# Double-buffering the token-tile operands of the K/V and Q projection loops

## The reference

```python
z = _layernorm(x)                       # (8, 2048, 1024), eps 1e-5
q, k, v = heads(Wq, bq), heads(Wk, bk), heads(Wv, bv)   # z @ W + b, 16 heads of 64
eq = jax.nn.elu(q)
ek = jax.nn.elu(k)
qn = eq / jnp.linalg.norm(eq, axis=-1, keepdims=True)
kn = ek / jnp.linalg.norm(ek, axis=-1, keepdims=True)
kv = jnp.einsum('bhsd,bhse->bhde', kn, v)
ctx = jnp.einsum('bhsd,bhde->bhse', qn, kv) / jnp.float32(math.sqrt(HD))
attn_out = _layernorm(ctx @ Wo + bo + z, g1, be1)
h = _gelu(attn_out @ W1 + b1)
out = _layernorm(h @ W2 + b2 + attn_out, g2, be2)
x = x + out                             # then a second layer: ternary-weight FFN with relu^2
```

## Time and profile before

| | us |
|---|---|
| median of the 2 runs shown | 6860.17 |
| lowest and highest of them | 6643.05, 7077.29 |
| the profiled execution's own time | 6654.75 |
| its span (slowest core, core 7) | 6653.2 |
| spans of the 8 cores | 6626.1 to 6653.2 |
| mean granted PE clock, all cores | 0.813 to 0.815 of full speed |

### The profile page before, as it was taken

How to read it: one execution, slowest core, us unless ns; L and a number is a source line. 1 busy time by engine, 2 the same in 40 slices (tenths; PEclk the granted TensorE clock), 3 DMA queues, 4 the chain that set the end, 5 groups by cost and what they waited for, 6 DMA issues and landing times.

```text
span 6653.2 us, 49468 instructions; the slowest of 8 cores (6626.1 to 6653.2 us)
## 1 busy us (share of the span) xinstructions
PE 3820.2 (57%) x16008; PEld 1598.1 (24%) x16008; DVE 1610.1 (24%) x2032; ACT 1075.9 (16%) x1151; POOL 169.4 (3%) x228
## 2 busy tenths in 40 slices
PE   1004555344458579699599599500001977768596
PEld 1001222121123034244134144000000322323232
DVE  2442222323330230120220220133233203121220
ACT  2000111112100121130130120221100403113040
POOL 0130000000000000000000000000000000000000
PEclk9998777677669789799799799755555998989899
DMA  2571000000000033143143132011221221212122
GB/s 91 173 232 68 0 0 0 29 0 0 0 26 0 0 87 94 44 97 96 40 90 100 40 91 85 0 65 65 73 63 40 52 50 51 50 47 53 45 54 57
DMA packets 649506, 374.35 MB, mean 56 GB/s; under 512 B 549328, under 2 KB 582304, under 8 KB 648240
## 3 DMA queue, kind: packets, MB, share of 16 engines
q1 hardware_dynamic: 629296, 304.07, 17.3%
q0 software_dynamic: 19968, 67.12, 3.2%
HBM read 312.39 MB, written 58.72 MB: 56 GB/s over the span
## 4 chain that ended last, share of the span: by engine, by line
PE 54%; DVE 16%; DMA 16%; issue 8%; ACT 6%; DVEq 1%; SPq 0%; ACTq 0%; POOLq 0%; POOL 0%
PE ps_p L1202 10%; PE ps_h L1140 10%; PE ps_h L1677 7%; PE ps_y L1748 5%; DMA ph8w<-spill_pj 4%; PE ps_q L489 3%; PE ps_v L489 3%; PE ps_wo L888 3%; PE ps_k L489 2%; DMA ph<-x 2%; PE ps_h L1680 2%; DMA spill_w1p<-phwp 2%; DMA spill_w2p<-phwp 2%; DMA strB<-wfc 2%; DMA spill_pj<-strB 2%
## 5 line engine op out<-in xcount | busy, mean ns | idle before, releaser
L1140 PE MATMUL ps_h<-ph 128*128 128x512 bf16 x3072 | 680.1, 382 | 51.0 <-DVE ph L1102 35.4
L1202 PE MATMUL ps_p<-strB,ph 128*128 128x512 bf16 x3072 | 674.2, 383 | 31.2 <-DMA ph<-spill_w2p 31.2
L1748 PE MATMUL ps_y<-strB,ph8w 128*128 128x512 bf16 x2048 | 491.8, 387 | 177.9 <-DMA ph8w<-spill_pj 138.1
L489 PE MATMUL ps_v<-ph1w,ph1zp 128*128 128x512 bf16 x768 | 201.5, 430 | 631.5 <-DVE ph1zp L479 631.5
L1677 PE MATMUL ps_h<-ph,ph8w 128*128 128x512 bf16 x2048 | 474.2, 385 | 14.3 <-DMA ph8w<-spill_fc 14.3
L1140 PEld LDWEIGHTS ps_h<-ph 128*128 128x128 bf16 x3072 | 296.6, 98 | 434.1 <-issue 94.8
L1202 PEld LDWEIGHTS ps_p<-strB,ph 128*128 128x128 bf16 x3072 | 302.8, 99 | 402.6 <-issue 48.0
L489 PE MATMUL ps_q<-ph1w,ph1zp 128*128 128x512 bf16 x768 | 201.9, 431 | 309.1 <-DVE ph1zp L479 309.1
L1694 ACT ACT_TABLE_LOAD x128 | 164.2, 1283 | 1069.1 <-PE ps_h L1680 1022.2
L1748 PEld LDWEIGHTS ps_y<-strB,ph8w 128*128 128x128 bf16 x2048 | 187.9, 99 | 483.2 <-issue 305.0
L1156 ACT ACT_TABLE_LOAD x128 | 164.2, 1283 | 735.2 <-PE ps_h L1140 735.2
(11 more groups left out here) (206 smaller groups left out, 3677.3 us busy)
## 6 DMA issues: line engine op xcount, KB each, us to landing
ph<-spill_w1p SPq DMA_DIRECT2D x256, 256.0 KB
ph<-spill_w2p SPq DMA_DIRECT2D x256, 256.0 KB
ph8w<-spill_fc SPq DMA_DIRECT2D x128, 256.0 KB
ph8w<-spill_pj SPq DMA_DIRECT2D x256, 128.0 KB
ph<-x SPq DMA_DIRECT2D x32, 512.0 KB
phwp<-w1t SPq DMA_DIRECT2D x32, 512.0 KB
spill_w1p<-phwp POOLq DMA_DIRECT2D x64, 256.0 KB, 3.9
phwp<-w SPq DMA_DIRECT2D x32, 512.0 KB
```

Of the source, the lines that this page charges most:

```text
L489: last = t.matmul(ps[:, cols], zz[:, k * 128:(k + 1) * 128], ww.rearrange("p (k w) -> p k w", k=ND)[:, k, cols], start=(pi == 0 and k == 0 ...
L1140: last = t.matmul(dst, ww[:, k * 128:(k + 1) * 128], aa[:, k, :], start=(pi == 0 and k == 0), stop=(pi == 2 and k == ND - 1))
L1202: last = t.matmul(ps_p2[:, n * 512:(n + 1) * 512], ww[:, n * 128:(n + 1) * 128], mm, start=(i == 0 and pi == 0), stop=False)
L1748: last = t.matmul(ps_y[:, jj * 512:(jj + 1) * 512], pjb[i % 2][:, jj * 128:(jj + 1) * 128], mm, start=(i == 0 and pi == 0), stop=(i == NF ...
```

## The change

- `zh`/`zl` get two buffers (`zpp`, `ph1zp` grows from 1024 to 2048 columns), one for even and one for odd tiles. The derive of tile `si + 1` moves ahead of the elu chain of tile `si` in DVE's list, behind the bias adds, and waits only for the projection that last read its buffer (`t_free`) in place of all matmuls.
- `kb` and `vb` get two buffers each; `bkb` moves from `B_t` to a tile of its own. `t_kv` keeps one count for each buffer.
- `e3` and `q3` are dropped: the max with 0 is done behind the exp and overwrites the buffer of the min, with a wait of its own, and the add follows.
- PE's wait on "s" ahead of a projection is dropped.
- SP gets a block that waits for the set-up's counts, and the loads of wv and wk lose their explicit wait for `v_z0`.

The diff, cut to its core:

```diff
+        setup_marks = {}
...
+        setup_marks["v"] = b.cnt["v"]
+        setup_marks["t"] = b.cnt["t"]
...
-        kb = B_t[:, 0:1024]
-        vb = B_t[:, 1024:2048]
-        e1 = B_t[:, 2048:3072]
-        e2 = B_t[:, 3072:4096]
-        e3 = B_t[:, 4096:5120]
+        kbp_ = [B_t[:, 0:1024], B_t[:, 2048:3072]]
+        vbp_ = [B_t[:, 1024:2048], B_t[:, 3072:4096]]
+        e1 = B_t[:, 4096:5120]
+        e2 = B_t[:, 6272:7296]
...
-                v.tensor_scalar(e1, blk, 0.0, None, ALU.min)
-                b.inc(v.tensor_scalar(e3, blk, 0.0, None, ALU.max), "v", 1)
+                b.inc(v.tensor_scalar(e1, blk, 0.0, None, ALU.min), "v", 1)
...
                 b.wait(v, "s", sv)
-                b.inc(v.tensor_add(e1, e2, e3), "v", 1)
+                b.inc(v.tensor_scalar(e1, blk, 0.0, None, ALU.max), "v", 1)
+                b.wait(v, "v")
+                b.inc(v.tensor_add(e1, e2, e1), "v", 1)
...
-        def derive_pair_blocks(zh, zl, si, v_ready):
+        def derive_pair_blocks(zh, zl, si, v_ready, t_free):
...
-            def _(v, v_ready=v_ready, t_e=t_e):
+            def _(v, v_ready=v_ready, t_free=t_free):
                 b.wait(v, "v", v_ready)
                 b.wait(v, "v")
-                b.wait(v, "t", t_e)
+                b.wait(v, "t", t_free)
                 b.inc(v.tensor_copy(zh3, srcs), "v", 1)
...
+            def _(sy):
+                b.wait(sy, "t", setup_marks["t"])
+                b.wait(sy, "v", setup_marks["v"])
+            block.sync(_)
+            v_wv = load_resident_w_pairs(wv_h, wv_l, wv_d, wtmp_kv)
+            v_wk = load_resident_w_pairs(wk_h, wk_l, wk_d, wtmp_kv)
-            v_wv = load_resident_w_pairs(wv_h, wv_l, wv_d, wtmp_kv, wait_v=v_z0)
-            v_wk = load_resident_w_pairs(wk_h, wk_l, wk_d, wtmp_kv, wait_v=v_z0)
...
+                dv[0] = derive_pair_blocks(zpp[0][0], zpp[0][1], 0, v_z0, 0)
...
                 for si in range(NT):
-                    sp, vp = derive_pair_blocks(zh, zl, si, v_z0)
-                    def _(t, si=si, v_evac_last=v_evac_last, sp=sp, vp=vp):
-                        b.wait(t, "v", max(v_wk, vp))
-                        b.wait(t, "s", sp)
+                    zh, zl = zpp[si % 2]
+                    def _(t, si=si, v_evac_last=v_evac_last, spvp=dv[si]):
+                        b.wait(t, "v", max(v_wk, spvp[1]))
                         if si >= 1:
                             b.wait(t, "v", v_evac_last)
                         tok_proj3(t, ps_v, wv_h, wv_l, zh, zl)
                         b.inc(tok_proj3(t, ps_k, wk_h, wk_l, zh, zl), "t", 1)
...
+                        v.tensor_add(vbp_[si % 2], ps_v[:], bvb)
+                        b.inc(v.tensor_add(kbp_[si % 2], ps_k[:], bkb), "v", 1)
                     v_evac_last = b.cnt["v"]
-                    v_elu[si] = elu_norm(kb)
+                    if si + 1 < NT:
+                        dv[si + 1] = derive_pair_blocks(
+                            zpp[(si + 1) % 2][0], zpp[(si + 1) % 2][1], si + 1,
+                            v_z0, t_proj[(si + 1) % 2])
+                    v_elu[si] = elu_norm(kbp_[si % 2])
```

More of the change, by code:

```diff
@@ L497, in build_program @@
         with nc.sbuf_tensor("ph1w", [128, 8192], F32) as WKV, \
-             nc.sbuf_tensor("ph1zp", [128, 1024], F32) as ZP:
+             nc.sbuf_tensor("ph1bias", [128, 1024], F32) as BKB, \
+             nc.sbuf_tensor("ph1zp", [128, 2048], F32) as ZP:
             WKVb = WKV[:].bitcast(BF16)
@@ L503, in build_program @@
             ZPb = ZP[:].bitcast(BF16)
-            zh, zl = ZPb[:, 0:1024], ZPb[:, 1024:2048]
+            zpp = [(ZPb[:, 0:1024], ZPb[:, 1024:2048]),
+                   (ZPb[:, 2048:3072], ZPb[:, 3072:4096])]
+            bkb = BKB[:]
             wtmp_kv = B_t[:, 0:2048]
@@ L575, in build_program @@
                 v_evac_last = 0
-                t_kv_last = 0
+                t_kv = [0, 0]
+                t_proj = [0, 0]
                 v_acc = 0
                 v_elu = [0] * NT
+                dv = [None] * NT
+                dv[0] = derive_pair_blocks(zpp[0][0], zpp[0][1], 0, v_z0, 0)
                 def emit_kv(si):
-                    nonlocal t_kv_last, v_acc
+                    nonlocal v_acc
                     def _(t, si=si, v_kn=v_elu[si], v_acc_=v_acc):
@@ L586, in _ @@
                             b.wait(t, "v", v_acc_)
+                        kb, vb = kbp_[si % 2], vbp_[si % 2]
                         last = None
@@ L597, in emit_kv, with _ @@
                     block.tensor(_)
-                    t_kv_last = b.cnt["t"]
-                    def _(v, si=si, tkv=t_kv_last):
+                    t_kv[si % 2] = b.cnt["t"]
+                    def _(v, si=si, tkv=t_kv[si % 2]):
                         b.wait(v, "t", tkv)
@@ L620, in build_program @@
                     block.tensor(_)
+                    t_proj[si % 2] = b.cnt["t"]
                     tp = b.cnt["t"]
@@ L624, in build_program, with _ @@
                         emit_kv(si - 1)
-                    def _(v, si=si, tp=tp, t_kv_last=t_kv_last):
+                    def _(v, si=si, tp=tp, tkv=t_kv[si % 2]):
                         b.wait(v, "t", tp)
                         b.wait(v, "ld", ld_b)
-                        b.wait(v, "t", t_kv_last)
-                        v.tensor_add(vb, ps_v[:], bvb)
-                        b.inc(v.tensor_add(kb, ps_k[:], bkb), "v", 1)
+                        b.wait(v, "t", tkv)
+                        v.tensor_add(vbp_[si % 2], ps_v[:], bvb)
+                        b.inc(v.tensor_add(kbp_[si % 2], ps_k[:], bkb), "v", 1)
                     block.vector(_)
                     v_evac_last = b.cnt["v"]
-                    v_elu[si] = elu_norm(kb)
+                    if si + 1 < NT:
[3 more added lines that the diff above has]
+                    v_elu[si] = elu_norm(kbp_[si % 2])
                 emit_kv(NT - 1)
@@ L652, in build_program @@
                 return nc
-            with nc.sbuf_tensor("ph1q", [128, 6400], F32) as PQ:
-                qbp = [PQ[:, 0:1024], PQ[:, 5376:6400]]
+            with nc.sbuf_tensor("ph1q", [128, 5376], F32) as PQ:
+                qbp = [PQ[:, 0:1024], PQ[:, 4352:5376]]
                 q1 = PQ[:, 1024:2048]
                 q2 = PQ[:, 2048:3072]
-                q3 = PQ[:, 3072:4096]
-                qrst = PQ[:, 4096:4224]
-                bq_pq = PQ[:, 4224:5248]
+                qrst = PQ[:, 3072:3200]
+                bq_pq = PQ[:, 3328:4352]
                 def elu_norm_q(blk):
@@ L667, in _ @@
                         b.wait(v, "v")
-                        v.tensor_scalar(q1, blk, 0.0, None, ALU.min)
-                        b.inc(v.tensor_scalar(q3, blk, 0.0, None, ALU.max), "v", 1)
+                        b.inc(v.tensor_scalar(q1, blk, 0.0, None, ALU.min), "v", 1)
                     block.vector(_)
@@ L680, in _ @@
                         b.wait(v, "s", sv)
-                        b.inc(v.tensor_add(q1, q2, q3), "v", 1)
+                        b.inc(v.tensor_scalar(q1, blk, 0.0, None, ALU.max), "v", 1)
+                        b.wait(v, "v")
+                        b.inc(v.tensor_add(q1, q2, q1), "v", 1)
                         b.wait(v, "v")
@@ L764, in emit_qtr, with _ @@
                         v_ev = b.cnt["v"]
+                    t_projq = [0, 0]
+                    dvq = [None] * NT
+                    dvq[0] = derive_pair_blocks(zpp[0][0], zpp[0][1], 0, v_kv, 0)
                     for si in range(NT):
[L767 to L771, removed]
+                        zh, zl = zpp[si % 2]
+                        def _(t, si=si, v_bias=v_bias, spvp=dvq[si]):
+                            b.wait(t, "v", max(v_wq, spvp[1]))
                             b.wait(t, "ld", ld_bq)
@@ L776, in build_program @@
                         block.tensor(_)
+                        t_projq[si % 2] = b.cnt["t"]
                         tp = b.cnt["t"]
@@ L787, in build_program @@
                         v_bias = b.cnt["v"]
+                        if si + 1 < NT:
+                            dvq[si + 1] = derive_pair_blocks(
+                                zpp[(si + 1) % 2][0], zpp[(si + 1) % 2][1], si + 1,
+                                v_kv, t_projq[(si + 1) % 2])
                         v_qn[si] = elu_norm_q(qbp[si % 2])
```

4 lines of the change are left out of this document (removed).

## The result

| us | before | after |
|---|---|---|
| median of all executions | 6878.01 (10) | 6314.3 (11) |
| lowest | 6643.05 | 6271.68 |
| the profiled execution's own time | 6654.75 | 6311.08 |
| its spans, lowest and highest core | 6626.1, 6653.2 | 6245.2, 6309.5 |
| ratio after to before | | 0.948, 95% interval 0.9435 to 0.9525 |

The medians of both kernels hold executions in which a die ran at a lower matrix clock for long, and the ratio leaves those out. The change makes the kernel 5.2% faster. The forecast was 6270 us, 0.942 of the profiled execution's 6654.75: the direction was right, the gain was forecast a little too large (385 us, while 0.948 leaves some 346), and 0.942 lies outside the measured interval. The range of 6225 to 6315 just holds the median of 6314.3; but set beside the median shown at the time, 6860.17, it ran from 0.907 to 0.921, and 0.948 is not in that.

What follows compares the result with a forecast made beforehand. PE was taken to wait at each K/V and Q handover for the derive queued behind the elu chain on DVE. Removing 194.9 us (K/V) and 189.9 (Q), 385 together, from 6654.75 gave 6270 us, range 6225 to 6315.

Steps and rivals of the forecast that it cites:

- The K/V loop: K/V handovers: the derive moved ahead of the elu chain removes 12.99 us from each of 15, 194.9 us.
- The cover: K/V loop: the 13 us chain hides under some 22.5 us of v and k matmuls, some 9 us to spare.
- The Q loop: Q handovers: 19.23 us for 31.93 in 14, with first handover and last tile 189.9 us removed.
- the rival limb: Q loop: the chain on DVE, 13.01 us, competes with PE's burst; it ends at 12.58 us from burst start.
- The clock at the start of a burst: Both loops: PE's idle shrinks from 18.6 to about 5.6 us, yet bursts start as slow as now, change 0.
- a rival with 5%: Both loops: the high clock survives the short idle, 32 us less, 6238 us; chance 5%.
- The weight loads: Set-up: they lose a wait that cost nothing and SP still issues right behind DVE's last copy; taken as 0.
- The sum: Both loops: 194.9 + 189.9 = 385 us off the profiled 6654.75, giving 6270 us.
- The dropped wait on "s": PE ahead of projections in 31 handovers: at most 0.1 us each, 0 to 3 us less; taken as 0.
- The clock under a denser load: All cores: rival that denser PE load brings a clock between the levels on the whole die, 6366 us; chance 3%.
- the estimate of 96 us: Both loops: by the skill's 13/16 limit, 16 tiles of 120 fast matmuls each take 0.05 us more per matmul.
- My range: Whole kernel: own range 6245 to 6300 us; widened to 6225 to 6315 to take in the high-clock rival, 88%.

Runs made afterwards that it cites:

- the overlapped version: Kernel after plus derive of tile si + 2 and accumulation or transpose copy inside the chain's waits, v taken out during k, two q PSUM buffers: ratio 0.9126.

## Why the prediction was right and where it was wrong

*The K/V loop:* right. Forecast 29.66 us a handover (42.65 less 12.99), measured 29.63 on core 7 and 29.6 to 29.8 on every core without the third level. The cover was there: the chain of a tile ends at 639.90 and `emit_kv`, which waits for it, starts at 650.54, 10.6 us later where some 9 were forecast, and without the chains the loop is no faster. Seen alone, 6460 us forecast and spans of 6460.2 to 6477.5 on the four unaffected cores.

*The Q loop:* right. Forecast 19.23 for 14 of the handovers, measured 19.24 on core 7 (1081.36 to 1350.68 us); with the shorter first one all 15 average 19.0 to 19.1 on the cores without the third level. The chain did become the rival limb. Its length with the moved max was forecast at 13.01 us and is 13.03. The Trainium skill (VectorE: DVE Perf Modes, section The DRAIN you can't avoid) says of a row of copies that the semaphore between them costs nothing extra; for this pair of operations the trace differs, if only by some 0.2 us. PE's second idle, before the transposes, is there in some tiles and up to 0.88 us long on core 7.

*The clock at the start of a burst:* right. The idle is 5.3 to 5.6 us and the next burst still starts at 1.2 GHz: the v halves of core 7 take 11.8 to 13.5 us and its k halves 10.5. That the high level outlasts the idle, a rival with 5%, didn't happen at these idles; in the overlapped version it held with no idle in K/V, and in some tiles of Q behind 2.84 us.

*The weight loads:* right. In the trace of after, on core 7, DVE's last copy ends 0.13 us before SP's first issue, to the hundredth as in the earlier trace rows, and the wv loads follow from 199.18 us on:

```profile
196.72 1.23 DVE L365 COPY strA<-ps_tr 128x1024 f32<-128x1024 f32 x1 [2.30 <-PE ps_tr L355]
198.08 0.33 SPq L53 DMA_DIRECT2D strB<-bv  x1
```

*The sum:* 385 us forecast, 383 found in the loops and 377 in the whole time, both without the third level. Of the 8 us, 2 are in the loops, 1 between them, and 5 were not placed. They are the smaller part of the miss: the eight executions of after that the ratio of 0.948 rests on average 6301.8 us, 32 over the forecast. The dropped wait on "s" was not tried alone; the handovers leave hardly 0.1 us for it.

*The clock under a denser load:* wrong, and this is the step that failed: the sum has no term for a clock between 1.2 and 2.4 GHz, and nothing was set aside for it in the range. I held the third level against the row in which 100 us of PE without a gap show 1.00 on core 7 and gave it 3%. That row was from an execution in which no core met the level, and one such execution can't tell how often it comes. Over all executions for which the cores' clocks are known, a die was below its usual clock in 26 of 32 of the kernel after and in 31 of 57 of the kernel before, some of them by very little. The profiled execution of after had it on four of eight cores, on two of these in both loops: 44 us in K/V and 12 in Q, so that the slowest core took 6309.5 us where core 0 took 6245.2. The time is that of the slowest of eight cores, so one pair is enough. With 377 us gained, an execution free of the level takes 6278 us, and the six of the kernel after in which no die was low took 6262.45 to 6291.9, 6278 on average. By the costs above, a pair caught in Q alone adds 12 and a pair caught in both loops 56, 6290 to 6334; the seven executions besides the profiled one in which no die was low for long took 6271.68 to 6331.62 us. The Trainium skill has the rule (TensorE: Matmul & The Clock Gate, section Seeing it yourself: a peak-current limit at 13/16, which depends on the data, and which zeros don't trip), and the traces agree with the level, 0.8125, and with the zeros. They disagree with its saying that the whole die goes there: pairs of cores do. Nor did the level stay while the load lasted: it left cores 4 and 5 at 732 us and came back at 833. So the estimate of 96 us by it was too high for the execution profiled, 56 us on the pair that was caught in both loops, as the level stood for 405 us and not for all of the bursts.

*My range* rested on bounds of single durations, 45 us to either side; it had no term for what the chip does to a pair of cores in some executions, though the two times shown, 6643.05 and 7077.29, were 6.5% apart and asked for one. A reading that changes nothing in the sum was wrong too: in the earlier trace rows the clock from slice 15 to the end of the MLP (slice 26) is not 0.9 and 1.0 throughout but falls to 7 and 8 tenths in five of the twelve slices.

*What stays open:* whether the change makes the third level more frequent (21 of 40 dies against 17 of 58), what it is in the data that brings the level, and what, besides the data, sets off a pair in one execution and not in the next. That zeros in the loops alone keep it out of the loops is likely after four executions, no more.

## What to carry to other kernels

Where a long chain on two engines stands between two bursts of a third, look at what the burst needs that is queued behind the chain: here two operations of 2 us together, moved ahead of 13 us of chain with a second buffer, gave 377 us in 30 handovers, and the next step (no burst waiting for anything but its own buffer) some 200 more. Such a sum from one trace can be right to some 2% and still miss the time of the slowest of eight cores: compare spans and mean granted clocks of all cores, over several executions, before a range is drawn around it.

## What the runs showed of the hardware

- The granted PE clock has a third level here, 0.8125 of full. 48 matmuls of 128x512 take 12.78 us at it and 10.52 at full.
- It is met by pairs of cores (0 and 1, 2 and 3, 4 and 5, 6 and 7) that can differ within a die: for cores 4 to 7 in one execution, 0.8125 for 430 us on the first pair and never on the second. It can leave a pair and come back under the same load (732 and 833 us on cores 4 and 5).
- It follows the data. With all large weights zero, 14 executions of both kernels (28 dies) were free of it, while 38 of the 84 dies of the executions with real weights beside them were low.
- It does not need dense loops: it was met with PE idle for over 18 us between bursts of 23 us, and four of thirteen executions of the version with 316 us of PE without a gap were free of it.
